# First attention of a four-part transformer kernel: normed rows turned in 32x32 blocks on VectorE and exchanged by transfers, in place of TensorE's transposes

## What is computed

```python
x = x + _L0_xattn_ref(_layernorm(x), ctx, Wq, Wk, Wv, Wo, gq, gk)   # 16 heads of 128, the part that is changed
x = x + _L0_ffn_ref(_layernorm(x), ...)                             # 512 -> 1024 -> 1024 -> 512
x = x + _L1_xattn_ref(_layernorm(x), ctx, pos, ...)                 # 32 heads of 16, rotary positions
x = x + _L1_ffn_ref(_layernorm(x), ...)                             # gated MLP and 8 of 1024 experts
```

```python
q = rmsnorm((h @ Wq).reshape(B, S, 16, 128), gq)
k = rmsnorm((ctx @ Wk).reshape(B, S, 16, 128), gk)
v = (ctx @ Wv).reshape(B, S, 16, 128)
out = softmax(q @ k.T / sqrt(128)) @ v        # for each head
return out.reshape(B, S, 2048) @ Wo
```

## Time and profile before

| | us |
|---|---|
| median of 3 runs | 1957.01 (1955.76 to 1959.29) |
| the profiled execution, its own time | 1958.99 |
| its span, first to last instruction | 1957.2 |
| TensorE busy | 1911.5 (98%) |
| VectorE busy | 1321.1 (67%) |
| ScalarE busy | 733.9 (37%) |
| GpSimd busy | 556.7 (28%) |
| DMA, mean over the span | 105 GB/s |

### The profile page before, as it was taken

One profiled execution on the slowest core, in us unless ns is written; L12 is line 12 of the kernel. 1 busy time (PEld: TensorE's weight loads), 2 busy tenths in 40 slices (PEclk: granted clock), 3 DMA queues, 4 the chain that ended last, 5 costly groups with the idle time before them and its releaser, 6 DMA issues. The chain is left out here.

```text
span 1957.2 us, 35844 instructions
## 1 busy us (share of the span) xinstructions
PE 1911.5 (98%) x13296; PEld 1540.1 (79%) x13296; DVE 1321.1 (67%) x2493; ACT 733.9 (37%) x2275; POOL 556.7 (28%) x705
## 2 busy tenths in 40 slices
PE   6999999999999999999999899999999999999999
PEld 5788888778888878888888677777688888888887
DVE  6666666765665654334263699998768787888786
ACT  5555545654555542111121445444433222122211
POOL 4323322322224335101021334343210223222221
PEclk9999999999999999999999899999999999999999
DMA  6553333543355442201032200000121645655554
GB/s 207 135 150 79 91 73 85 152 109 99 99 137 146 104 121 90 76 11 54 11 98 75 64 20 26 19 21 30 42 92 54 193 158 196 206 194 166 193 168 159
DMA packets 157015, 205.62 MB, mean 105 GB/s; under 512 B 23537, under 2 KB 111601, under 8 KB 156913
## 3 DMA queue, kind: packets, MB, share of 16 engines
q1 hardware_dynamic: 133200, 117.26, 21.6%
q0 software_dynamic: 23712, 87.04, 13.7%
HBM read 136.61 MB, written 17.30 MB: 79 GB/s over the span
## 5 line engine op out<-in xcount | busy, mean ns | idle before, releaser
L2387 POOL DMA_INDIRECT m_ring<-in_table,m_row x128 | 125.6, 981 | 372.0 <-DVE l_x_all L2500 272.0
L48 PE MATMUL four_banks<-l_yT_hi,m_hi 128*128 128x512 f32 x512 | 199.4, 390 | 0.0
L48 PE MATMUL four_banks<-l_yT_lo,m_hi 128*128 128x512 f32 x512 | 199.2, 389 | 0.0
L533 ACT ACTIVATE prob<-four_banks,mx,rms 128x128 f32<-128x128 f32 x256 | 121.6, 581 | 171.4 <-DVE mx L671 171.4
L1149 DVE TENSOR_SCALAR f_relu<-bank,f_b 128x512 f32<-128x512 f32 x64 | 48.0, 749 | 163.6 <-ACT f_h_hi L1092 163.6
L1092 ACT ACTIVATE f_h_hi<-bank,f_b 128x512 fp32r<-128x512 f32 x64 | 44.1, 689 | 257.2 <-PE bank L48 257.2
L335 POOL TENSOR_TENSOR rms<-ssq,constants 128x4 f32<-128x4 f32 x128 | 27.2, 213 | 394.9 <-ACT junk_k L521 277.3
L338 POOL TENSOR_TENSOR rms<-rms,constants 128x4 f32<-128x4 f32 x128 | 129.8, 1014 | 10.0
L48 PEld LDWEIGHTS four_banks<-l_yT_hi,m_hi 128*128 128x128 f32 x512 | 96.1, 188 | 20.3 <-issue 0.2
L48 PEld LDWEIGHTS four_banks<-l_yT_lo,m_hi 128*128 128x128 f32 x512 | 96.1, 188 | 19.7
L2364 ACT ACTIVATE m_act_of<-m_dot,l_ln_y 128x2 f32<-128x2 f32 x64 | 18.9, 296 | 239.6 <-DVE m_junk L2490 239.6
(11 more groups left out here) (314 smaller groups left out, 5286.9 us busy)
## 6 DMA issues: line engine op xcount, KB each, us to landing
qkT<-blocks SPq DMA_DIRECT2D x256, 128.0 KB, 2.7
pT_sb<-dealt SPq DMA_DIRECT2D x256, 64.0 KB, 2.1
f_stage<-in_w POOLq DMA_DIRECT2D x14, 512.0 KB, 4.6
f_x_in<-x SPq DMA_DIRECT2D x18, 256.0 KB, 3.1
ctx_in<-in_ctxT SPq DMA_DIRECT2D x32, 128.0 KB, 2.6
x_in<-in_x SPq DMA_DIRECT2D x16, 256.0 KB, 3.2
x<-xres SPq DMA_DIRECT2D x16, 256.0 KB, 2.8
x<-l_x_all SPq DMA_DIRECT2D x16, 256.0 KB, 2.1
```

The costliest lines, as they stand in the source:

```text
L48: mm = pe.matmul(out, st, mv, start=first and n == 0, stop=last and n == len(terms) - 1)
L533: a = act.activation(prob[g][:, j, :].rearrange("q (b a) -> q a b", b=4), scores, ACT.Exp, bias=mx[g][:, 1, j:j + 1], scale=rms[g][:, 0, j ...
L2387: pool.indirect_dma_start(ring[slot][:], None, table, bass.IndirectOffsetOnAxis(ap=row[:, tile_of(g), k:k + 1], axis=0)).then_inc(S[f"got{ ...
```

## The change

In steps with s + 2 of at least 2 (so for 30 of the 32 rows of steps), xn is no longer transposed by TensorE. VectorE turns xn in 32x32 blocks into `dealt` (`turn_x`, between the keys' and the queries' turn of group 1), and SP sends the blocks back into xn with four transfers (`send_x`, between `send(s + 1, 0)` and `send(s + 1, 1)`). ScalarE and VectorE split the result from xn instead of from bank 2, and both do so later in their order: ScalarE behind the copies of the values and the context's split, VectorE behind `split_o(s, 1)`. The blocks arrive with the features of each 128 in another order (4j + b in place of 32b + j), so the rows of Wq are laid out in that order on the host; the first two rows of steps, still transposed by TensorE, are written in the same order by the layer norm. The layer norm no longer waits for TensorE's transposes from the third row on. `normalise` waits for x_sent in place of p_loaded1 before it fills `dealt` again.

```diff
--- before.py
+++ after.py
@@ -151,7 +151,7 @@
     den = [sb(f"den{g}", [P, 2, G], F32) for g in range(2)]
 
     names = """ident_loaded x_loaded ctx_loaded xres_loaded0 xres_loaded1 xres_loaded2 xres_loaded3 xres_loaded4
-        g_loaded stats_ready ln_eps ln_ready xn_ready xT_turned xT_hi xT_lo ctx_hi ctx_split set stored eps_added
+        g_loaded stats_ready ln_eps ln_ready xn_ready xT_turned x_blocks x_sent xT_hi xT_lo ctx_hi ctx_split set stored eps_added
         s_turn y_begun y_ready y_added wq0_staged wv_staged wk_staged wq1_staged wo0_staged wo1_staged""".split()
     names += [f"{n}{g}" for g in range(2) for n in """q_made k_made v_made q_blocks k_blocks qk_loaded v_copied q_squared
         k_squared q_rms k_rms scored bias_ready exped p_blocks p_loaded mixed oT_hi oT_lo""".split()]
@@ -166,6 +166,18 @@
     def there(s):
 
         return not isinstance(s, int) or 0 <= s < STEPS
+
+    def in_blocks(s):
+
+        return not isinstance(s, int) or 2 <= s < STEPS
+
+    def raw_xT(s):
+        if in_blocks(s):
+            return xn[:].rearrange("d (p k i) -> d k p i", p=4, k=KD)
+        return bank[2][:].rearrange("d (k p i) -> d k p i", k=KD, p=4)
+
+    def in_tokens(xT):
+        return xT[:].rearrange("d k (p i) -> d k p i", p=4)
 
     def flat(w):
         return w[:].rearrange("p k w -> p (k w)")
@@ -260,6 +272,12 @@
             for p in range(4):
                 sp.dma_start(qkT[g][:, p].rearrange("d h i -> d (h i)"),
                              blocks[g][32 * p:32 * (p + 1)].rearrange("j b h i -> j b (h i)")).then_inc(S[f"qk_loaded{g}"], 16)
+
+        def send_x(s):
+            sp.wait_ge(S["x_blocks"], s - 1)
+            for p in range(4):
+                sp.dma_start(xn[:, p * P:(p + 1) * P], dealt[32 * p:32 * (p + 1)].rearrange("j b h i -> j b (h i)")
+                             ).then_inc(S["x_sent"], 16)
 
         def deal(s, g):
             sp.wait_ge(*at(f"p_blocks{g}", s))
@@ -292,6 +310,9 @@
                 ahead["loads"](sp, now)
             if there(s + 1):
                 send(s + 1, 0)
+            if in_blocks(s + 2):
+                send_x(s + 2)
+            if there(s + 1):
                 send(s + 1, 1)
             if storing and now != STEPS:
                 store(s - 1)
@@ -390,16 +411,13 @@
         all_steps(pool, step, roots=True)
 
     def tensor(pe, ahead):
-        def turn(out_bank, src, what):
-            for j in range(4):
-                t = pe.transpose(bank[out_bank][:, j * P:(j + 1) * P], src[:, j * P:(j + 1) * P], ident[:])
-            t.then_inc(S[what], 1)
-
         def turn_x(s):
             if isinstance(s, int) and s == 0:
                 pe.wait_ge(S["ident_loaded"], 16)
             pe.wait_ge(*at("xn_ready", s))
-            turn(2, xn, "xT_turned")
+            for k in range(KD):
+                t = pe.transpose(bank[2][:, k * P:(k + 1) * P], xn[:, k * P:(k + 1) * P], ident[:])
+            t.then_inc(S["xT_turned"], 1)
 
         def queries(s, g):
             if g == 0:
@@ -483,7 +501,7 @@
                 pe.wait_ge(*at("q_blocks0", s + 1))
                 pe.wait_ge(*at("q_squared0", s + 1))
                 ahead["turn_x"](pe, 0, 1)
-            if there(s + 2):
+            if there(s + 2) and not in_blocks(s + 2):
                 turn_x(s + 2)
             if there(s + 1):
                 values(s + 1, 0)
@@ -501,10 +519,13 @@
 
     def scalar(act, ahead):
         def split_xT(s):
-            act.wait_ge(*at("xT_turned", s))
+            if in_blocks(s):
+                act.wait_ge(S["x_sent"], 64 * (s - 1))
+            else:
+                act.wait_ge(*at("xT_turned", s))
             if there(s - 1):
                 act.wait_ge(*at("q_made1", s - 1))
-            act.activation(flat(xTp[0]), bank[2][:], ACT.Copy).then_inc(S["xT_hi"], 1)
+            act.activation(in_tokens(xTp[0]), raw_xT(s), ACT.Copy).then_inc(S["xT_hi"], 1)
 
         def split_ctx(s):
             act.wait_ge(S["ctx_loaded"], 16 * (s + 1))
@@ -586,8 +607,6 @@
                 split_o(s, 0)
             if now == STEPS - 2:
                 ahead["split_x_hi"](act, 0, 1)
-            if there(s + 2):
-                split_xT(s + 2)
             if now is not None and AHEAD_FROM < now <= AHEAD_FROM + 4:
                 ahead["split_hi"](act, now - AHEAD_FROM - 1)
             if there(s):
@@ -599,6 +618,7 @@
                 copy_v(s + 1, 1)
             if there(s + 2):
                 split_ctx(s + 2)
+                split_xT(s + 2)
             if now == NB - 2:
                 split_hi(act, "wq0", 1)
             if now in (0, NB):
@@ -628,14 +648,17 @@
             dve.bn_aggr(mv[:], bn[:]).then_inc(S["stats_ready"], 1)
 
         def layer_norm(s, first_half):
-            if there(s - 1):
+            if isinstance(s, int) and s in (1, 2):
                 dve.wait_ge(*at("xT_turned", s - 1))
             kept = ln[:].rearrange("p b c -> p (b c)")[:, bass.ds((s % NB) * 2, 2)]
             if first_half:
                 dve.wait_ge(*at("ln_ready", s))
                 dve.tensor_copy(kept, mv[:])
-                dve.tensor_scalar(xn[:], xres[:].rearrange("p b d -> p (b d)")[:, bass.ds(s * DM, DM)], mv[:, 0:1], mv[:, 1:2],
-                                  ALU.subtract, ALU.mult).then_inc(S["xn_ready"], 1)
+                out, row = xn[:], xres[:].rearrange("p b d -> p (b d)")[:, bass.ds(s * DM, DM)]
+                if not in_blocks(s):
+                    out = out.rearrange("p (k j b) -> p k b j", k=KD, b=4)
+                    row = row.rearrange("p (k b j) -> p k b j", k=KD, b=4)
+                dve.tensor_scalar(out, row, mv[:, 0:1], mv[:, 1:2], ALU.subtract, ALU.mult).then_inc(S["xn_ready"], 1)
             else:
                 dve.wait_ge(S["x_loaded"], 16 * (s - NB + 1))
                 then(dve.tensor_copy(ln_now[:], kept))
@@ -644,10 +667,15 @@
 
         def split_xT(s):
             dve.wait_ge(*at("xT_hi", s))
-            dve.tensor_tensor(flat(xTp[1]), bank[2][:], flat(xTp[0]), ALU.subtract).then_inc(S["xT_lo"], 1)
+            dve.tensor_tensor(in_tokens(xTp[1]), raw_xT(s), in_tokens(xTp[0]), ALU.subtract).then_inc(S["xT_lo"], 1)
 
         def blocks_of(heads):
             return heads.rearrange("p (h b i) -> p b h i", h=G, b=4)
+
+        def turn_x(s):
+            dve.wait_ge(*at("xn_ready", s))
+            dve.wait_ge(S["p_loaded1"], 64 * (s - 1))
+            dve.transpose(dealt[:], blocks_of(xn[:])).then_inc(S["x_blocks"], 1)
 
         def turn_q(s, g):
             dve.wait_ge(*at(f"q_made{g}", s))
@@ -678,7 +706,10 @@
             if g == 1:
                 dve.wait_ge(S["p_loaded0"], 64 * (s + 1))
             elif there(s - 1):
-                dve.wait_ge(S["p_loaded1"], 64 * s)
+                if in_blocks(s + 1):
+                    dve.wait_ge(S["x_sent"], 64 * s)
+                else:
+                    dve.wait_ge(S["p_loaded1"], 64 * s)
             dve.transpose(dealt[:], blocks_of(flat(prob[g]))).then_inc(S[f"p_blocks{g}"], 1)
 
         def split_o(s, g):
@@ -744,6 +775,8 @@
                 norm_and_turn_k(s + 1, 1)
             if now == FIRST:
                 split_lo(dve, "wv0", 0)
+            if in_blocks(s + 2):
+                turn_x(s + 2)
             if there(s + 1):
                 turn_q(s + 1, 1)
             if now == FIRST:
@@ -764,14 +797,14 @@
             if now in (0, NB):
                 split_lo(dve, "wo0", now // NB)
                 split_o(s, 1)
-            if there(s + 2):
-                split_xT(s + 2)
             if now == NB - 2:
                 split_lo(dve, "wk1", 1)
             if first_half:
                 statistics(s + 3)
             if there(s) and now not in (0, NB):
                 split_o(s, 1)
+            if there(s + 2):
+                split_xT(s + 2)
             if now == NB - 2:
                 split_lo(dve, "wq0", 1)
             if now in (0, NB):
@@ -2651,7 +2684,7 @@
         "ident": np.eye(P, dtype=np.float32),
         "x": np.asarray(x).reshape(T, DM),
         "ctxT": np.asarray(ctx_1024).reshape(T, KC, P).transpose(2, 1, 0),
-        "wq0": halves(L0_xattn_Wq), "wk0": halves(L0_xattn_Wk), "wv0": halves(L0_xattn_Wv),
+        "wq0": halves(np.asarray(L0_xattn_Wq).reshape(4, 4, 32, 2048).transpose(0, 2, 1, 3).reshape(DM, 2048)), "wk0": halves(L0_xattn_Wk), "wv0": halves(L0_xattn_Wv),
         "wo0": np.asarray(L0_xattn_Wo).reshape(2, 1024, DM),
         "gq": on_rows(np.asarray(L0_xattn_gq)), "gk": on_rows(np.asarray(L0_xattn_gk)),
         "w1": np.asarray(L0_ffn_W1).T, "w2": np.asarray(L0_ffn_W2).T, "w3": np.asarray(L0_ffn_W3).T,
```

## The result

The changed kernel takes 1981.95 us (median of 4, 1978.61 to 1982.73) against 1957.05 us: a ratio of 1.0124, 95% interval 1.0109 to 1.0139, so 24.9 us slower. The forecast was 1975.7, with a range of 1970 to 1985. Sign, mechanism and range held; the loss is 6 us larger than the forecast's 18.7.

A forecast was written before the change was run, and what follows sets the result against it. TensorE's order and the chain to oT_lo were taken as equally long bounds. 30 turns at 0.64 us make 19.2, less 1.3 spare, less 0.2, plus 1.0 prologue: +18.7 us, 1975.7 us, range 1970 to 1985.

The forecast's parts named there:

- The bound: First attention's steps: TensorE's order and the chain to oT_lo are equally long bounds, spare some 0.045 us on average.
- Rival A: TensorE is the bound and VectorE's idle time hides the turn: 12.2 us won, 1944.8 us; chance 5%.
- the signs that I had named: Expected in the changed kernel's trace: steps of 21.7 us, TensorE waiting for oT_lo about 1.1 us each, some 30 in all.
- Part 2: VectorE's turn of xn ahead of the queries' turn: 0.64 us a step, no wait for dealt; bounds 0.64 to 1.08.
- Parts 4 and 5: xn's four transfers on SP's queue and the later xT_hi, xT_lo splits: hidden, by 3 us and 1.2 us of cover.
- Rival B: xn's blocks land late, delaying xT_hi, xT_lo and the reduction: 2006 us for one us a step beyond the cover; chance 6%.
- Part 7: Prologue: the second row's split moves behind the context's, so the first reduction starts later: +1.0 us, once.
- Rival C: TensorE's clock falls after the new stall in each step, 1.7 us each, 51 in all: 2027 us; chance 3%.

The follow-up runs named there:

- the run with another buffer: The changed kernel with xn's blocks turned into the second probability buffer instead of dealt; 1978.00 us, ratio 1.0102.
- the kernel with VectorE's part alone: The kernel before plus VectorE's turn of xn, its result unread, without transfers and with TensorE's transposes kept; 1976.22 us, ratio 1.0093.
- the last variant: The changed kernel with oT_hi first, turn behind the queries' turn, probability buffer, xn's transfers last and splits in the next step; 1949.01 us, ratio 0.9955.

## Why the prediction came out as it did

**The bound.** Right, and shown from three sides: less work on TensorE alone changes nothing, a shorter chain alone changes nothing, and both together give 0.44 us a step. Rival A, which put its point at a spare of 1.08 us, is out. A table of waits with 1.2 us for oT_lo between 60 and 700 us (the kernel before) did not tell this; the 0.01 us between oT_lo's end with its hand-over and its use did. Of the signs that I had named, the sum of the waits came out lower than the 30 us: 22.5 us between 60 and 700, since TensorE is idle 0.76 us in a plain step and not 1.07.

**Part 2, the price of the turn.** Forecast 0.64 us, measured 0.58 in the plain step: the turn of xn is followed by the next turn 0.59 us after its start. Less the spare, 0.54 us a step was measured on the average against 0.595 forecast. In 25 steps this makes 13.6 us where my sum has 14.9.

**Part 2, the wait for dealt.** This is the step that failed. I wrote that the last transfer lands at 279.84 and the turn starts at 280.30, "so no wait", and kept 1.08 us as the upper end, from the landings of transfers issued between 149.8 and 341.1 us, where no weights are loaded. In step 15 a landing took 6.3 us and the turn waited 2.73 us; the step lost 5.00 us instead of 0.64. That is 4.4 us above the forecast for this step, and nearly all of the 4.6 us by which the two spans differ from my sum (the medians differ from it by 6.2); the run with another buffer gave 3.6 of them back. The trace of the kernel before has a landing of 5.6 us in this very step. I had even noted that VectorE is the bound in step 15, and did not ask what a new wait in that place would meet.

**Parts 4 and 5, the transfers and the later splits.** Hidden in plain steps, as forecast. Not in steps with loads: steps 1 to 3 lost 3.2 us in place of 1.8. In step 2 the turn waited 0.57 us for dealt. The probabilities' own turn waited 0.79 us for dealt in step 2 and 1.40 in step 3, where it was 0.52 and 0.72. "Hidden by 3 us" for the transfers of group 1 had no cover to spare there: in the variants in which the step is shorter or the turn later, the scores stood up to 3.4 us for them. Where they stood over 1.3 us, the last of them was issued near a load or behind it and landed after 5.6 to 7.1 us instead of 2.7, and so 3 us of cover were too few. Rival B named a queue as the cause but the wrong transfer: not xn's own landing was late, the one queued behind it was.

**Part 7, the prologue.** Forecast 1.0 us, measured 0.54. The order is as forecast: the copy of the values, the context's split, xT_hi (31.57), xT_lo (32.20), and the first reduction right behind it at 32.80. Only the second copy of the values came 0.45 us earlier, at 30.77 instead of 31.22. It is also a small number against its spread: the kernel with VectorE's part alone has its first reduction at 32.64, with the prologue unchanged.

**Rival C, the clock.** Right to set low for plain steps: 1.00 in all of them, with a stall of 0.76 us in each. It did cost something in step 15, where the stretch at the lower level doubled, from 3.4 to 6.8 us. It doubled as well in the run with the turn alone, so the wait for dealt is not the only thing that lengthens it. The stalls of 1.3 and 1.0 us from which I argued were not both for late weights: the second was for turned keys (row `blocks L664` of the earlier trace rows).

**Luck in the sum.** Two parts of the difference stand nowhere in my sum and nearly cancel: step 30 gave 1.46 us back, and the time behind the first attention grew by 1.8 us. In step 16, where I had put the whole turn, 0.24 us was measured.

**Left open.** From step 31's reduction to the end the changed kernel's profile is 1.8 us longer (1260.1 against 1258.3). It has more time at the lower clock there: by the clock record 13.7 us around 1115 us and 3.4 us around 1422 us, against 10.2 us around 1095 us before. Over the profiles of all ten kernels this stretch takes 1256.9 to 1260.1 us, with the same code in it. Why it shifts with what ran ahead of it was not tried.

## What to carry to other kernels

Where an engine is 98% busy, look at how early its inputs are ready before counting on its work: here 0.01 us of spare meant that 13 us of saved matmuls were worth nothing, and an instruction put ahead of a chain's member cost nearly its full time, while 1.7 us of idle time lay behind the next one. Moving work to another engine needed the chain relieved in the same edit here, and the pair was worth more than the sum of its parts. A new wait or a transfer put into a queue must be priced in the steps where the queue is crowded, not in the plain one: two of the variants lost there what they had won in twenty plain steps. The trace of the kernel before shows such a step: transfers issued behind a load landed late in it already, where nothing waited for them.

## What the runs showed of the hardware that I had not expected

VectorE's subtraction that makes xT_lo took 0.68 us in the kernel before, with a bank as source. From xn in SBUF it took 0.93 us in the changed kernel's plain step (294.38 to 295.31), while GpSimd worked from 294.02 to 294.76, and 0.69 us in the last variant, at another place in the step. It was hidden either way, so its cause was not tried. A transfer of 64 KB between partitions, which lands 2.1 us after its issue in nearly all cases, took 6.3 us in step 15 of the changed kernel, issued 0.54 us behind a load of 1 MB by another queue. In the kernel before three such transfers, issued 0.06 to 1.35 us behind the load of that step, took 5.0 to 5.6 us. A transfer of 128 KB (queries and keys), which takes 2.6 us at the median between 150 and 350 us in the kernel before, took 7.1 us when it was issued 0.27 us behind a load. What in the transfers' way makes them late was not tried.
